# Windowed attention and a ternary feed-forward: values taken ahead of scores, projections a slot sooner, chunk 4's feed-forward in the loop

## The reference

```python
qkv = xp @ w_qkv
sim = jnp.einsum('bhnid,bhnjd->bhnij', qw, kw)      # per block of 16 queries
sim = jnp.where(mask[None, None], mask_value, sim)
attn = stable_softmax(sim, axis=-1)
attn = jnp.einsum('gh,bhnij->bgnij', w_th, attn)    # mixes the heads
out = jnp.einsum('bhnij,bhnjd->bhnid', attn, vw)
x = _layernorm(x + (out @ w_out + b_out))
h = jax.nn.gelu(_ternary_linear(x, w_up), approximate=False)
x = _layernorm(x + _ternary_linear(h, w_down))
```

## Time and profile before

| | us |
|---|---|
| runs before, median of 3 (lowest to highest) | 242.18 (241.50 to 242.18) |
| the profiled execution | 243.09 |
| its span, from first to last instruction | 241.3 |
| PE matmul busy | 226.1 |
| VectorE busy | 176.6 |
| ScalarE busy | 164.1 |
| GpSimd busy | 92.6 |

### The profile page before, as it was taken

One profiled execution on the slowest core, in us unless ns is written; L12 is line 12 of the kernel. 1 busy time (PEld: TensorE's weight loads), 2 busy tenths in 40 slices (PEclk: granted clock), 3 DMA queues, 4 the chain that ended last, 5 costly groups with the idle time before them and its releaser, 6 DMA issues.

```text
span 241.3 us, 10011 instructions
## 1 busy us (share of the span) xinstructions
PE 226.1 (94%) x4343; PEld 203.1 (84%) x4343; DVE 176.6 (73%) x461; ACT 164.1 (68%) x311; POOL 92.6 (38%) x111
## 2 busy tenths in 40 slices
PE   7999899999999999999999999999999989989970
PEld 7899789888999999888988998888988977889750
DVE  0674699987777882688766885688468999785864
ACT  2686466776666648985599559964898334988652
POOL 7035204531343342444515454536254353120542
PEclk9999999999999999999999999999999999999975
DMA  6937560020020001100200111010201001000002
GB/s 217 293 101 209 165 139 7 7 61 3 3 58 13 24 3 39 35 21 8 65 3 4 48 34 36 3 46 4 68 3 29 20 3 46 1 4 22 3 3 87
DMA packets 19107, 11.69 MB, mean 48 GB/s; under 512 B 2232, under 2 KB 18168, under 8 KB 18936
## 3 DMA queue, kind: packets, MB, share of 16 engines
q1 hardware_dynamic: 18324, 10.47, 15.3%
q10 hardware_dynamic: 740, 0.59, 0.8%
HBM read 8.91 MB, written 2.10 MB: 46 GB/s over the span
## 4 chain that ended last, share of the span: by engine, by line
PE 57%; DVE 15%; ACT 8%; issue 7%; POOL 6%; SPq 2%; DMA 2%; POOLq 0%; DVEq 0%; ACTq 0%
PE bank L1108 9%; PE bank L1110 8%; PE bank L1109 8%; PE bank L1257 7%; PE bank L1231 6%; PE bank L1215 4%; DVE CTl L876 4%; POOL gTl L533 2%; DVE AT L881 2%; POOL xw L506 2%; DMA raw<-in_L_attn_x 2%; SPq L395 2%; DVE sm L896 2%; PE bank L1327 2%; PE bank L1189 2%
## 5 line engine op out<-in xcount | busy, mean ns | idle before, releaser
L577 ACT ACTIVATE Yb<-bank 128x512 f32<-128x512 f32 x64 | 38.4, 601 | 28.4 <-PE bank L1110 27.9
L519 POOL TENSOR_TENSOR E<-E,rc 128x400 f32<-128x400 f32 x32 | 27.9, 871 | 77.3 <-DVE rc L898 77.3
L876 DVE TENSOR_TENSOR CTl<-bank,CTh 128x512 fp32r<-128x512 f32 x64 | 41.1, 683 | 22.3 <-ACT CTh L577 22.1
L1108 PE MATMUL bank<-xTh,Gh 128*128 128x256 f32 x128 | 39.4, 308 | 1.7 <-ACT Yb L577 1.5
L1108 PE MATMUL bank<-CTh,Mh 128*128 128x256 f32 x128 | 37.0, 289 | 0.6 <-DVE CTl L876 0.6
L577 ACT ACTIVATE CTh<-bank 128x512 fp32r<-128x512 f32 x64 | 34.8, 600 | 2.5 <-PE bank L1257 2.4
L1110 PE MATMUL bank<-CTh,Ml 128*128 128x256 f32 x128 | 36.1, 282 | 0.0
L724 ACT ACTIVATE E<-E 128x400 f32<-128x400 f32 x32 | 17.3, 541 | 27.5 <-DVE E L890 27.4
L1109 PE MATMUL bank<-CTl,Mh 128*128 128x256 f32 x128 | 36.0, 281 | 0.0
L1109 PE MATMUL bank<-xTl,Gh 128*128 128x256 f32 x128 | 35.8, 280 | 0.0
L1110 PE MATMUL bank<-xTh,Gl 128*128 128x256 f32 x128 | 35.7, 279 | 0.0
(11 more groups left out here) (142 smaller groups left out, 469.3 us busy)
## 6 DMA issues: line engine op xcount, KB each, us to landing
raw<-in_L_attn_x SPq DMA_DIRECT2D x37, 64.0 KB
pt_rows<-PT SPq DMA_DIRECT2D x2, 512.0 KB, 4.7
R<-pt_rows SPq DMA_DIRECT2D x1, 1024.0 KB, 5.6
xr<-in_L_attn_x SPq DMA_DIRECT2D x6, 128.0 KB
out<-y SPq DMA_DIRECT2D x6, 128.0 KB, 1.9
raw<-in_L_attn_x SPq DMA_DIRECT2D x13, 56.0 KB
w_sb<-in_L_attn_w_qkv SPq DMA_DIRECT2D x2, 256.0 KB, 4.7
w_sb<-in_L_attn_w_qkv ACTq DMA_DIRECT2D x2, 256.0 KB, 4.5
```

The source lines that it names most:

```text
L519: tt(e, e, rc[s % 2][:, :].unsqueeze(2).broadcast_to([P, TILES, WIN]), ALU.mult).then_inc(s_norm, 1)
L577: copy = lambda o, i, **k: nc.scalar.activation(o, i, ACT.Copy, **k)
L876: v.tensor_tensor(ct_view(CTl[s // 4 % 2], s % 4, q), c_view(s, q), ct_view(f32(CTh[s // 4 % 2][:, :, :]), s % 4, q), ALU.subtract).then_i ...
L1108: mm(o, wh, rh, start=start, stop=False, **k)
```

## The change

In the loop, from slot TURN = 7 on, the values of slot s-2 come first, then the scores of s, then the transposes of s-1 (they were those of s-2), so that the values of a slot stand one slot behind its transposes. Slot 7 does values and transposes once more to get there. ScalarE and VectorE take the copies in the same order. The projection is one slot sooner (O_LAG 6): slot 7 does (0, 0) and (0, 1), slot 31 does (6, 1) and (6, 2). Each chunk's feed-forward starts a slot sooner too (FIRST 10), and chunk 4 has its own in the loop, to k = 5. GELU comes behind the exponential and ahead of the second Yb copy. The square sums stand among the scores, ahead of the mask. VectorE takes in the normed rows behind the shift. GpSimd's rows_high comes a slot later, behind `normalise`. Behind the loop the order is another on all engines, chunk 4 is gone from it but for its last steps, values use their own banks throughout, and keep_busy issues 4, 4 and 14 matmuls for 5.

The diff, less the hunks on banks and on waits that follow from the new order:

```diff
--- before.py
+++ after.py
...
@@ -56,7 +56,8 @@
 LAG = 2
-O_LAG = 7
+O_LAG = 6
+TURN = 7
 NT = B * N // P
@@ -279,19 +280,20 @@
-            if s < 28:
-                return [divmod(s - O_LAG, 4)] if s >= O_LAG else []
-            return {28: [(5, 1), (5, 2)], 29: [(5, 3)], 30: [(6, 0)], 31: []}[s]
-
-        FIRST = [11 + 4 * n for n in range(5)] + [30]
+            if s < TURN:
+                return []
+            early = {7: [(0, 0), (0, 1)], 31: [(6, 1), (6, 2)]}
+            return early.get(s, [divmod(s - O_LAG, 4)])
+
+        FIRST = [10 + 4 * n for n in range(6)]
...
-            return [(n, s - first) for n, first in enumerate(FIRST) if -1 <= s - first < (9, 9, 9, 9, 5, 1)[n]]
-
-        UP_BANK = {5: (0, 2), 6: (0, 2), 7: (6, 5)}
+            return [(n, s - first) for n, first in enumerate(FIRST) if -1 <= s - first < (9, 9, 9, 9, 6, 1)[n]]
+
+        UP_BANK = {5: (1, 0), 6: (2, 0), 7: (6, 5)}
         AT_BANK = {7: 5}
-        XT_BANK = {5: 4, 7: 5}
+        XT_BANK = {5: 2, 7: 5}
         DN_BANK = {5: 4, 6: 3, 7: 0}
...
@@ -545,7 +544,7 @@
                 for n, k in ffn(s):
-                    if k == 4 and n < 4:
+                    if k == 4:
                         hidden_low(n, 0)
@@ -556,16 +555,17 @@
                         last_root(n)
-                if s % 4 == 1 and s < STEPS - 4:
-                    rows_high((s + 3) // 4)
+                if s == 1:
+                    rows_high(1)
+                if s % 4 == 2 and 2 < s < STEPS - 4:
+                    rows_high((s + 2) // 4)
                 if s % 4 == 0 and s > 0:
...
+            last_root(4)
             variance_roots(6)
             variance_roots(7)
-            hidden_root(4)
             hidden_root(5)
-            last_root(4)
             hidden_root(6)
@@ -679,11 +679,11 @@
                 o = slice(2 * t, 2 * t + 2)
-                if n < 4:
+                if n < 5:
                     act.wait_ge(f_gl, 2 * n + t + 1)
...
                     act.wait_ge(f_gl, 12)
-                elif n > 5:
+                elif n > 6:
                     act.wait_ge(f_ss, n - 1)
@@ -705,24 +705,33 @@
                 if s == FIRST[0] - 1:
                     act.wait_ge(s_small, 32)
-                if s > LAG:
+                if LAG < s <= TURN:
                     ct_hi(s - LAG - 1)
-                if 0 < s < O_LAG:
+                if 0 < s < TURN:
                     y_out(s, 0)
-                if s >= LAG:
+                if LAG <= s <= TURN:
                     at_hi(s - LAG)
-                if s == 0 or s >= O_LAG:
+                if s == 0 or s == TURN:
                     y_out(s, 0)
-                if s < O_LAG:
+                if s >= TURN:
+                    ct_hi(s - 2)
+                    at_hi(s - 1)
+                if s > TURN:
+                    y_out(s, 0)
+                if s < TURN:
                     y_out(s, 1)
                 for n, k in ffn(s):
-                    if k == 4 and n < 4:
+                    if k == 4:
                         squares(n, 0)
                         squares(n, 1)
...
                 act.wait_ge(s_sub, s + 1)
                 nc.scalar.activation(e, e, ACT.Exp).then_inc(s_exp, 1)
-                if s >= O_LAG:
+                for n, k in ffn(s):
+                    if k == 2:
+                        gelu(n, 0)
+                        gelu(n, 1)
+                if s >= TURN:
                     y_out(s, 1)
                 if s < len(IN_STEP):
@@ -730,46 +739,34 @@
                 for n, k in ffn(s):
-                    if k == 4 and n < 4:
+                    if k == 4:
                         down_out(n)
...
                         x1_hi(n)
-                    if k == 3 and n < 4:
+                    if k == 3:
                         hidden_high(n, 0)
                         hidden_high(n, 1)
-                    if k == 2 and n < 4:
-                        gelu(n, 0)
-                        gelu(n, 1)
-                    if k == 8 and n < 3:
+                    if k == 8:
                         result(n)
-            at_hi(30)
-            ct_hi(29)
-            gelu(4, 0)
+            ct_hi(30)
             at_hi(31)
-            ct_hi(30)
-            gelu(4, 1)
-            ct_hi(31)
             x1_hi(5)
             stage(6)
-            hidden_high(4, 0)
-            hidden_high(4, 1)
-            squares(4, 0)
-            squares(4, 1)
+            ct_hi(31)
             gelu(5, 0)
...
             hidden_high(5, 1)
-            result(3)
             x1_hi(6)
+            result(4)
             squares(5, 0)
             stage(7)
+            squares(5, 1)
             gelu(6, 0)
...
             hidden_high(6, 1)
-            down_out(4)
-            squares(5, 1)
             down_out(5)
...
@@ -1005,41 +1001,36 @@
                 if s == LAG + 1:
                     dve.wait_ge(s_pt, 32)
-                if s > LAG:
+                if LAG < s <= TURN:
                     ct_lo(s - LAG - 1)
-                if s >= LAG:
+                if LAG <= s <= TURN:
                     at_lo(s - LAG)
+                if s > TURN:
+                    ct_lo(s - 2)
+                shift(s)
+                if s == TURN:
+                    ct_lo(s - 2)
                 for n, k in ffn(s):
-                    if k == 5 and n == 3:
+                    if k == 5:
+                        dve.wait_ge(f_back, n + 1)
                         hidden_sum(n)
+                if s >= TURN:
+                    at_lo(s - 1)
                 for n, k in ffn(s):
                     if k == 1:
                         input_scale(n)
                         up_input(n)
-                shift(s)
-                for n, k in ffn(s):
-                    if k == 5 and n < 3:
-                        hidden_sum(n)
-                    if k == 5 and n == 3:
-                        second_sum(n)
-                    if k == 6 and n == 3:
-                        second_norm(n)
-                    if k == 0 and n == 5:
-                        residual(n)
-                if s == STEPS - 1:
-                    input_scale(5)
-                    up_input(5)
                 if s < 2:
                     absolute_sum(s)
...
                 if s == 3:
                     ternary(0)
-                if 4 <= s < O_LAG:
+                if 4 <= s < TURN:
                     fills(IN_STEP[s - 1][-1:])
                 total(s)
                 for n, k in ffn(s):
-                    if k == 5 and n < 3:
+                    if k == 5 and n < 4:
                         second_sum(n)
                     if k == 7:
@@ -1055,45 +1046,42 @@
                 for n, k in ffn(s):
-                    if k == 0 and n < 5:
+                    if k == 0:
                         residual(n)
-                    if k == 6 and n < 3:
+                    if k == 6:
                         second_norm(n)
-            at_lo(30)
-            ct_lo(29)
+            input_scale(5)
+            up_input(5)
+            ct_lo(30)
             at_lo(31)
-            ct_lo(30)
+            x1_lo(5)
+            second_sum(4)
             ct_lo(31)
-            x1_lo(5)
+            second_norm(4)
             residual(6)
-            hidden_low(4, 0)
-            hidden_low(4, 1)
+            result_shift(4)
+            hidden_low(5, 0)
             input_scale(6)
             up_input(6)
-            hidden_low(5, 0)
             hidden_low(5, 1)
...
             hidden_low(6, 1)
+            hidden_sum(5)
             input_scale(7)
-            hidden_sum(4)
             up_input(7)
-            second_sum(4)
+            second_sum(5)
             x1_lo(7)
-            hidden_sum(5)
-            second_norm(4)
-            second_sum(5)
+            second_norm(5)
             hidden_sum(6)
             hidden_low(7, 0)
-            second_norm(5)
             hidden_low(7, 1)
-            result_shift(4)
             second_sum(6)
+            result_shift(5)
             hidden_sum(7)
             second_norm(6)
-            result_shift(5)
             second_sum(7)
@@ -1216,7 +1204,7 @@
-            def scores(s):
+            def scores(s, sums=()):
@@ -1230,6 +1218,9 @@
                         mm(bank[S_BANK][lo:lo + 32, WIN * tile:WIN * tile + WIN], Yb[s // 4 % 2][:, ytile, lo:lo + 32], keys,
                            start=(tile == 0), stop=False, skip_group_check=True)
+                for n in sums:
+                    pe.wait_ge(f_dS, n + 1)
+                    square_sum(n)
                 if s % (2 * SLOTS) == 0:
                     ins = mm(bank[S_BANK][:, 0:TILES * WIN], sel[:, :], mask[:, :], start=False, stop=True, skip_group_check=True)
@@ -1242,10 +1233,7 @@
                 pe.wait_ge(s_ATl, s + 1)
-                need(pe, s_CTl, 60 if s == 31 else 2 * s if s < 30 else 0)
-                if s == 30:
-                    pe.wait_ge(s_sub, STEPS)
-                    pe.wait_ge(s_Ye, 64)
```

(70 more changed lines are left out.)

## The result

The changed kernel takes 239.3 us (median of 4 runs, 238.57 to 240.3) against 241.84: a ratio of 0.9898 with a 95% interval of 0.9859 to 0.9938. Twelve more runs in a later comparison gave 240.2 against 241.7, 0.9923 (0.9894 to 0.9952). So it is faster, by 1.5 to 2.5 us. The forecast was 6.2 us faster, 236.0, in a range of 232.0 to 240.8: the median lies in the range and the sign is right, but the gain is less than half of the forecast. The profiled execution took 240.3, with a span of 238.5.

What follows compares the result with a forecast made beforehand. PE's instruction list plus its waits bound the kernel. Terms -3.4, -0.6 (square sums inside the scores), -3.8, +3.0, +2.3, -2.5 and -1.2 sum to -6.2 us, giving 236.0 us from 242.18, range 232.0 to 240.8.

Steps and rivals of the forecast that it cites:

- What bounds the kernel: Whole kernel: PE's list of instructions plus PE's waits set the time; 0.95 us in each four slots is waiting.
- The change of shape: Slots 8 to 27: three changes of array shape for four, 0.17 us saved in each of 20 slots, -3.4 us.
- Rival 1: Every slot: entering 32 columns costs 0.17 us whatever stood before, so no shape saving; +3.4, 239.4 us, 18%.
- The old waits: Four-slot feed-forward stretches: early GELU ends PE's waits for Yb and GpSimd's gTl, 4 x 0.95, -3.8 us.
- The new waits: Transposes wait for rows 0.25 us after GELU and 0.5 where the next chunk is normed; +3.0 us (0 to +6).
- Work drawn forward: Before slot 28: slot 7's second projection (1.42) and slot 8's earlier values (0.9) add 2.3 us, paid back later.
- Slot 28 to the last projection: From slot 28's mask to the last projection's end: 31.8 us for 34.3, -2.5 us (0 to -4).
- After the last projection: From there to the end: 1.6 us moves out, fillers and square sums cost 0.4; -1.2 us, nothing counted for the clock.
- Rival 2: Slots 28 to the end: VectorE and ScalarE's tables set slots 28 to 31, clock falls as early; +3.7, 239.7 us, 12%.
- Rival 3: Loop slots: no new waits, the hand-overs and the 0.5 us are hidden; -3.0, 233.0 us, 10%.
- Rival 4: Every slot: PE waits for GpSimd, as the four-engine loop with 0.8 us to spare becomes the limit; +10, 246 us, 12%.

Runs made afterwards that it cites:

- the fillers: Changed kernel with 14 more matmuls that nobody reads, ahead of the values of slot 28: 239.1 us, ratio 0.9893 to the kernel before.
- two single moves: Kernel before with transposes behind the scores and GELU ahead of the second Yb copy: 238.8 us, ratio 0.9860.
- four amendments: Changed kernel: 14 unread matmuls before slot 28's values, result one slot later, x1n before AT's low half, none before chunk 6's down, 7's up; 236.6 us.

## Why the prediction was right or wrong

*What bounds the kernel.* PE's list does in plain slots. It doesn't in the slots with feed-forward, where I took it as the limit too: there the list and the chain of copies have nearly the same length, so each is worth its gain only while the other has slack. The kernel before shows it: with the transposes behind the scores, its plain slots got 0.2 us shorter each, and its slots with feed-forward on the whole did not.

*The change of shape, -3.4.* The size was right, even small (5.42 to 5.22). The rule that the prediction took from the Trainium skill, TensorEngine Tiling (Array Packing), section Tiling Modes, that a change of the tiling mode drains the engine, agrees: values to scores was one such change like any other (0.90 us). Rival 1 fell, though its 239.4 us happens to be what was measured. In the kernel before the saving was worth nothing that the median shows (0.9 us in slots 8 to 28), and about 1 with GELU early. What it is worth alone in the changed kernel was not found, since undoing it brings the wait for rows.

*The old waits, -3.8.* The mechanism holds: GELU early alone took 3.0 out of slots 8 to 28, and 2.1 of the median. The sum counted it in full beside the shape. In the changed kernel both can stand in full, by the sum below; that this is so because the feed-forward's copies come earlier in a slot too was not tried.

*The new waits, +3.0.* Right in places and size: 0.25 us for E in each slot behind GELU (1.0 in 4), x1n 0.5. The places missed are two small ones, AT ahead of the values of the slot behind GELU (0.2) and x1n without a result ahead of it, in slot 11.

*Slots 8 to 28 together.* These terms say -4.8, measured were -3.5. The rest is a step that was left out: the whole feed-forward starts a slot sooner, not the projection alone. So chunk 3's square sums and way back and chunk 4's transposes of x1n, 0.7 and twice 0.25, come ahead of slot 28's mask. With them the terms say -3.6. "Work drawn forward" had slot 7 and 8 only: +2.3, measured +2.1.

*Slot 28 to the last projection, -2.5.* This is the step that failed: +0.1, 2.6 us off. 1.5 is the fall of the clock, shown by the fillers. The prediction had the wait for AT behind it (1.9 said, 1.99 measured) and thought of the clock for the end only, although the wait was in its own list; here it put the fall at nothing. The rest is PE's list. The waits come to some 3.7 us for the 4.0 of the sum, so the list is about 29.2 for 27.8. Read off the timeline, the transposes stand there five times and not four, since those of slot 27 come behind slot 28's mask (0.4). Each of five value parts has a change of shape ahead of it too (from 187.20 to 187.40, where full matmuls start 0.12 apart: 0.08), and behind transposes the second full matmul comes as late after the first; these small pieces make up most of what is left.

*After the last projection, -1.2.* Measured -1.4, but that it fits is luck. Chunk 7's low halves no longer stand around a norm, and PE waits 0.41 us for the second of them, not 0.75. Against that its up starts 7.6 us behind the last projection for 6.9, so what stands ahead of it costs 0.7 and not 0.4. The large part is the clock, for which nothing was counted: the last square sums take 0.71 for 1.03. Below is the line of the changed kernel, then that of the kernel before with GELU early:

```profile
230.95 0.71 PE L1311 MATMUL bank<-ones,gT 128*32 128x1 f32 x64
229.13 0.71 PE L1328 MATMUL bank<-ones,gT 128*32 128x1 f32 x64
```

The second kernel has the old order and the old five fillers there. In its profiled execution the clock fell behind these square sums, at 230.8, and the stretch took 20.0 us for the 21.1 of the kernel before; with the transposes behind the scores it was 19.9. So 1.1 to 1.2 of the 1.4 us is the moment at which the clock fell in one execution of the kernel before, and the new order gave 0.2 to 0.3. Whether the 22 fillers hold the clock isn't shown: with the old order and five fillers it stayed up through the last square sums in two of four profiled executions, and with the new order and five in the only one.

*Rivals.* Rival 2 said that the end gives nothing, since VectorE and ScalarE's tables set slots 28 to 31. Its 239.7 is near what was measured, and its middle stretch did give nothing, but not by its mechanism: the wait for AT was 2.8 us and not over 3, the end took 19.7 and not 21, and with the clock held up PE was through 1.5 us sooner, so PE and not the copies set the rest. Rival 3 (no new waits) fell. Rival 4 did not come but was as near as its 0.8 us of slack.

*The rest of the change.* Chunk 4 in the loop, the shorter pipeline and the new order at the end were not tried one by one. But the kernel before with two single moves has 0.9860, and the whole change 0.9898 and 0.9923: taken together, the rest gave nothing that can be told and may have cost up to 1.5 us as it stands (the intervals overlap). With four amendments it comes to 0.9783. Whether it is needed for that is not shown, as the amendments were not tried on the kernel before with the two moves; the fillers at slot 28 only mend a wait that the change brought.

## What to carry over

Where two chains are nearly as long, don't add their gains: a saving on PE came back in good part as waits until ScalarE's order was mended, so look for which copy would be late next before counting. The wait of 2 us on PE was not only its own length: price the clock behind such a wait, and try matmuls that nobody reads in its place. Before a difference at the end of two profiles is put down to the order, see in both when the clock fell. And when a pipeline is made shorter by a slot, list all that moves ahead of each mark, and put what nobody waits for, as an old result, behind what the next slot needs.

## What the hardware showed that was not expected

One stretch from 191.24 to 193.23 us with PE idle was followed by 3.4 us at a granted clock of 0.50 (194.16 to 197.57), though PE had been busy up to it and was busy again for 0.9 us before the clock fell. PE lost 1.5 us by it. The same came in five of five profiled executions with this wait. In the kernel before, PE's waits of 0.64, 0.38 and 0.36 between 197 and 207 us had no such fall behind them. And at the end, where kernels before the change run one and the same order, the clock fell ahead of the last square sums in two profiled executions and behind them in two, which is worth 0.8 to 1.2 us.
